# Flamingo layer, attention stage: masked maximum in one VectorE operation, scores in three passes over high and low halves, four probability buffers, new engine orders

## The reference

```python
xn = _ln(x, g_x, b_x)                        # also ln, from the latents (here x)
q = ln @ w_q
kv_in = jnp.concatenate([xn, ln], axis=1)    # 120 + 256 = 376 rows
k, v = jnp.split(kv_in @ w_kv, 2, axis=-1)
q, k, v = (split(q) * scale, split(k), split(v))
sim = jnp.einsum('bhid,bhjd->bhij', q, k)
sim = jnp.where(m, sim, -jnp.finfo(sim.dtype).max)   # m: the mask over the 120 context rows, True after them
attn = jax.nn.softmax(sim, axis=-1)
out = jnp.einsum('bhij,bhjd->bhid', attn, v)
return _ln(out @ w_out, g_o, b_o)
```

## Time and profile before

| | us |
|---|---|
| median of 3 runs | 2430.0 (2428.2 to 2432.1) |
| profiled execution, its own time | 2407.8 |
| span of the profiled execution | 2405.8 |
| PE, DVE, ACT, POOL busy | 2280, 1685, 1278, 1002 |

### The profile page before, as it was taken

One profiled execution on the slowest core, in us unless ns is written; L12 is line 12 of the kernel. 1 busy time (PEld: TensorE's weight loads), 2 busy tenths in 40 slices (PEclk: granted clock), 3 DMA queues, 4 the chain that ended last, 5 costly groups with the idle time before them and its releaser, 6 DMA issues. The chain is left out here.

```text
span 2405.8 us, 53171 instructions
## 1 busy us (share of the span) xinstructions
PE 2280.3 (95%) x15744; PEld 1885.0 (78%) x15744; DVE 1685.0 (70%) x5052; ACT 1278.3 (53%) x3249; POOL 1001.6 (42%) x1418
## 2 busy tenths in 40 slices
PE   4999999999999999999949999999789999999998
PEld 3777777777777777777649999999768888888887
DVE  2577676776767776777645555555378989898997
ACT  3666666666666666676523333333244445454554
POOL 1455555556556555555530000000155555555552
PEclk9999999999999999999979999999999999999999
DMA  7001001011010010010033222221122211111110
GB/s 279 19 28 36 26 29 37 18 35 33 22 36 27 27 36 26 29 37 13 22 118 105 80 80 80 80 80 45 57 67 59 60 58 59 58 58 58 58 48 19
DMA packets 111772, 128.97 MB, mean 54 GB/s; under 512 B 15058, under 2 KB 98505, under 8 KB 111424
## 3 DMA queue, kind: packets, MB, share of 16 engines
q1 hardware_dynamic: 99264, 105.42, 13.8%
q0 software_dynamic: 12288, 21.21, 3.1%
HBM read 84.42 MB, written 54.53 MB: 58 GB/s over the span
## 5 line engine op out<-in xcount | busy, mean ns | idle before, releaser
L367 POOL TENSOR_TENSOR a_prob<-a_prob,a_rden 128x752 f32<-128x752 f32 x256 | 369.0, 1442 | 321.1 <-DVE a_rden L647 300.1
L641 DVE TENSOR_REDUCE a_nmax<-a_score 128x1 f32<-128x376 f32 x512 | 270.7, 542 | 187.1 <-PE a_score L964 176.7
L496 ACT ACTIVATE a_prob<-a_score,a_nmax 128x376 f32<-128x376 f32 x512 | 292.6, 574 | 94.2 <-DVE a_nmax L641 94.2
L1292 ACT ACTIVATE e_hidden<-e_first,e_b 128x256 f32<-128x256 f32 x320 | 133.9, 471 | 287.2 <-PE e_first L80 283.9
L972 PE MATMUL a_turned<-a_ident,a_prob 128*128 128x128 f32 (+1 forms) x1536 | 238.0, 281 | 32.2 <-DVE a_probT L653 20.7
L972 PEld LDWEIGHTS a_turned<-a_ident,a_prob 128*128 128x128 f32 (+1 forms) x1536 | 170.9, 142 | 99.2 <-issue 57.3
L80 PE MATMUL e_first<-e_rowsT,e_w 128*128 128x256 f32 x1920 | 238.7, 285 | 1.6 <-issue 1.6
L80 PE MATMUL e_second<-e_w,e_hidden 128*128 128x256 f32 x1920 | 239.7, 285 | 0.0
L80 PEld LDWEIGHTS e_first<-e_rowsT,e_w 128*128 128x128 f32 x1920 | 235.0, 194 | 1.8 <-issue 1.8
L960 PE MATMUL a_score<-a_kT,a_qT 64*128 64x376 f32 x1024 | 231.9, 530 | 2.4 <-ACT a_prob L496 2.3
L80 PEld LDWEIGHTS e_second<-e_w,e_hidden 128*128 128x128 f32 x1920 | 232.7, 192 | 0.0
(11 more groups left out here) (203 smaller groups left out, 4859.5 us busy)
## 6 DMA issues: line engine op xcount, KB each, us to landing
slots<-a_y SPq DMA_DIRECT2D x8, 1280.0 KB, 14.3
e_rows<-slots SPq DMA_DIRECT2D x40, 256.0 KB, 4.0
answers<-e_y SPq DMA_DIRECT2D x40, 256.0 KB, 2.3
a_xn<-x SPq DMA_DIRECT2D x32, 256.0 KB
w_in<-W SPq DMA_DIRECT2D x16, 512.0 KB, 3.9
a_xr<-x SPq DMA_DIRECT2D x32, 256.0 KB, 2.9
x<-a_x SPq DMA_DIRECT2D x32, 256.0 KB, 3.1
e_w_in<-W SPq DMA_DIRECT2D x16, 512.0 KB, 4.1
```

Source lines behind the costliest of these rows:

```text
L367: nc.gpsimd.tensor_tensor(prob[:, u % 4], prob[:, u % 4], rden[:, u % 4].unsqueeze(2).to_broadcast([P, 2, NKV]), ALU.mult) \
L496: nc.scalar.activation(prob[:, u % 4, a], score[SCORE_AT[u][a]][:, 0:NKV], ACT.Exp, bias=nmax[:, u % 4, a:a + 1], accum_out=den[:, u % 4, ...
L641: nc.vector.tensor_reduce(nmax[:, u % 4, a:a + 1], score[SCORE_AT[u][a]][:, 0:NKV], AX.X, ALU.max, negate=True).then_inc(nmax_ok[a], 1)
L1292: nc.scalar.activation(hidden[:, 2 * j + i], first[:, j, i * CH:(i + 1) * CH], ACT.Relu, bias=b1[:, 2 * j + i, bass.ds(e, 1)]).then_inc(re ...
```

## The change

- Keys and queries get two planes, high and low, in fp32r. ACT writes the high one as before, DVE the low one with two new functions, `k_low` (four per batch, 128x376) and `q_low` (two per batch, 128x512). What waited for `k_hi` and `q_hi` on PE now waits for `k_lo` and `q_lo`.
- `scores` makes three fp32r passes per head in place of one f32 matmul, the heads in turn; the bf16 matmul for the mask and `firstrow` go.
- The mask row is f32, 376 wide, zero beyond the context. `row_max` becomes one `tensor_tensor_reduce`: it adds the mask to the scores, negates, writes the result to `prob` in SBUF and its minimum to `nmax`. `exps` then reads `prob` (scale -1) and not PSUM. So the score bank is free after `row_max`, and `scores` waits for `nmax_ok` and not for `exp_ok`; `row_max`, which now writes the buffer, waits for the transposes of the unit four earlier, as `exps` did.
- The orders in `step` are new on PE, DVE, ACT and POOL. Among it: `turn_x` is done for batch s at the end of step s, not for s - 1 near the start; `times_v` of pair 2 moves from the end of a step to behind the scores of unit 2 in the next; on DVE `stat` moves forward, `logits_shift` into the next step, `place` forward, and `over_sum(s - 1, 0)` from the end of a step into the next, which makes `logits_in` the last operation of a step; on ACT `standardise` moves forward; on POOL `norm0` moves forward and `dispatch` ahead of the eighth `normalise`.

```diff
@@ -146,8 +145,8 @@
         xh = sb("a_xh", [P, 3, D])
         kvin = sb("a_kvin", [P, KD, NKV])
         kvin2 = sb("a_kvin2", [P, 2, 2, KD, NKV], F32R)
-        qT = sb("a_qT", [P, 2, KI, S])
-        kT = sb("a_kT", [P, 2, KI, NKV])
+        qT = sb("a_qT", [P, 2, 2, KI, S], F32R)
+        kT = sb("a_kT", [P, 2, 2, KI, NKV], F32R)
         vo = sb("a_vo", [P, 2, 3, KI, 2, DH])
...
                 eng.wait_ge(nmax_ok[a], NG * b + u + 1)
-                at_least(eng, turned_ok[a], NG * b + u - 3)
-                nc.scalar.activation(prob[:, u % 4, a], score[SCORE_AT[u][a]][:, 0:NKV], ACT.Exp,
-                                     bias=nmax[:, u % 4, a:a + 1],
+                nc.scalar.activation(prob[:, u % 4, a], prob[:, u % 4, a], ACT.Exp,
+                                     bias=nmax[:, u % 4, a:a + 1], scale=-1.0,
                                      accum_out=den[:, u % 4, a:a + 1]).then_inc(exp_ok[a], 1)
 
...
+            def k_low(b, p, m):
+                eng.wait_ge(k_hi, KI * b + m + 1)
+                nc.vector.tensor_tensor(kT[:, p, 1, m], work[0][:, 0:NKV], kT[:, p, 0, m].bitcast(F32),
+                                        ALU.subtract).then_inc(k_lo, 1)
+
+            def q_low(b, p, i):
+                eng.wait_ge(q_hi, 2 * b + 2 - i)
+                pair = slice(2 * i, 2 * i + 2)
+                nc.vector.scalar_tensor_tensor(qT[:, p, 1, pair], work[1][:].rearrange("p (m s) -> p m s", m=2),
+                                               DH ** -0.5, qT[:, p, 0, pair].bitcast(F32),
+                                               ALU.mult, ALU.subtract).then_inc(q_lo, 1)
+
             def mask_line(b, p):
+                if isinstance(b, int) and b == 0:
+                    eng.wait_ge(small_in, 16 * N_SMALL)
                 for a in range(2):
-                    at_least(eng, score_ok[a], NG * (b - 1))
-                nc.vector.tensor_scalar(mask_row[:, p], mask_u8[:, bass.ds(b, 1)].rearrange("p o c -> p (o c)"),
+                    at_least(eng, nmax_ok[a], NG * (b - 1))
+                nc.vector.tensor_scalar(mask_row[:, p, 0:C], mask_u8[:, bass.ds(b, 1)].rearrange("p o c -> p (o c)"),
                                         -1.0, MASKED, ALU.add, ALU.mult).then_inc(mrow_ok, 1)
 
-            def row_max(b, u, a):
-
+            def row_max(b, p, u, a):
+
+
+                at_least(eng, turned_ok[a], NG * b + u - 3)
+                if u == 0:
+                    eng.wait_ge(mrow_ok, b + 1)
                 eng.wait_ge(score_ok[a], NG * b + u + 1)
-                nc.vector.tensor_reduce(nmax[:, u % 4, a:a + 1], score[SCORE_AT[u][a]][:, 0:NKV], AX.X,
-                                        ALU.max, negate=True).then_inc(nmax_ok[a], 1)
+                by_itself(eng, waited)
+                nc.vector.tensor_tensor_reduce(prob[:, u % 4, a], score[SCORE_AT[u][a]][:, 0:NKV], mask_row[:, p],
+                                               -1.0, 3.0e38, ALU.add, ALU.min,
+                                               nmax[:, u % 4, a:a + 1]).then_inc(nmax_ok[a], 1)
...
             def step(s, p):
...
+                if live(s - 2):
+                    row_max(s - 2, p, 1, 1)
                 if live(s - 3):
                     turned_out(s - 3, 6, 1)
                 if live(s - 2):
-                    row_max(s - 2, 1, 1)
-                    row_max(s - 2, 2, 0)
+                    row_max(s - 2, p, 2, 0)
+                    over_sum(s - 2, 0)
+                    row_max(s - 2, p, 2, 1)
                 if live(s - 3):
                     att_low(s - 3, 2)
                     turned_out(s - 3, 7, 1)
-                if live(s - 1):
-                    mask_line(s - 1, q)
-                if live(s - 2):
+                if live(s - 2):
+                    row_max(s - 2, p, 3, 1)
+                    row_max(s - 2, p, 3, 0)
                     over_sum(s - 2, 1)
...
                 if live(s - 4):
                     place(s - 4, p)
-                if live(s - 1):
-                    row_max(s - 1, 1, 0)
+                if live(s - 2):
+                    att_low(s - 2, 1)
+                    turned_out(s - 2, 4, 1)
+                if live(s - 1):
+                    row_max(s - 1, q, 0, 0)
+                    k_low(s - 1, q, 2)
+                if live(s):
+                    mask_line(s, p)
+                if live(s - 1):
+                    row_max(s - 1, q, 0, 1)
+                if live(s - 2):
+                    turned_out(s - 2, 5, 1)
+                    over_sum(s - 2, 7)
+                if live(s - 1):
+                    row_max(s - 1, q, 1, 0)
                 if live(s - 3):
                     logits_in(s - 3)
-                    logits_shift(s - 3)
-                if live(s - 1):
-                    over_sum(s - 1, 0)
...
 
                 m, i = u // 2, u % 2
-                if u == 0:
-                    eng.wait_ge(mrow_ok, b + 1)
                 if i == 0:
-                    eng.wait_ge(k_hi, KI * b + m + 1)
-                    eng.wait_ge(q_hi, 2 * (b + 1))
-                at_least(eng, exp_ok[0], NG * b + u)
-                at_least(eng, exp_ok[1], NG * b + u - 1)
-                for a in range(2):
-                    rows = slice(64 * a, 64 * a + 64)
-                    nc.tensor.matmul(score[SCORE_AT[u][a]][:, 0:NKV], qT[rows, p, m, i * P:(i + 1) * P],
-                                     kT[rows, p, m], start=True, stop=False)
-                for a in range(2):
-                    rows = slice(64 * a, 64 * a + 64)
-                    nc.tensor.matmul(score[SCORE_AT[u][a]][:, 0:C], firstrow[rows], mask_row[rows, p],
-                                     start=False, stop=True).then_inc(score_ok[a], 1)
+                    eng.wait_ge(k_lo, KI * b + m + 1)
+                    eng.wait_ge(q_lo, 2 * (b + 1))
+                at_least(eng, nmax_ok[0], NG * b + u)
+                at_least(eng, nmax_ok[1], NG * b + u - 1)
+                for w, (plane_q, plane_k) in enumerate(PASSES):
+                    for a in range(2):
+                        rows = slice(64 * a, 64 * a + 64)
+                        made = nc.tensor.matmul(score[SCORE_AT[u][a]][:, 0:NKV],
+                                                qT[rows, p, plane_q, m, i * P:(i + 1) * P], kT[rows, p, plane_k, m],
+                                                start=w == 0, stop=w == len(PASSES) - 1)
+                        if w == len(PASSES) - 1:
+                            made.then_inc(score_ok[a], 1)
...
                 if live(s - 2):
                     scores(s - 2, p, 2)
                 if live(s - 3):
+                    times_v(s - 3, q, 2)
+                    turn_prob(s - 3, 7, 0)
+                if live(s - 2):
+                    scores(s - 2, p, 3)
+                if live(s - 3):
                     turn_prob(s - 3, 7, 1)
-                    turn_prob(s - 3, 7, 0)
-                if live(s - 2):
+                if live(s - 2):
+                    project_k(s - 2, p, 3)
+                if live(s - 1):
+                    turn_c(s - 1)
+                if live(s - 2):
+                    turn_prob(s - 2, 0, 0)
+                    turn_prob(s - 2, 0, 1)
                     project_v(s - 2, p, 1)
-                if live(s - 1):
-                    turn_c(s - 1)
-                    turn_x(s - 1)
-                if live(s - 2):
-                    turn_prob(s - 2, 0, 1)
-                    scores(s - 2, p, 3)
-                    turn_prob(s - 2, 0, 0)
+                    scores(s - 2, p, 4)
                 if live(s - 3):
                     times_v(s - 3, q, 3)
...
+                    turn_prob(s - 2, 4, 0)
+                if live(s - 1):
+                    project_k(s - 1, q, 2)
                     scores(s - 1, q, 0)
-                if live(s - 2):
-                    turn_prob(s - 2, 4, 0)
+                    project_v(s - 1, q, 2)
+                if live(s - 3):
+                    router_turn(s - 3, q)
+                if live(s - 2):
                     turn_prob(s - 2, 5, 1)
-                if live(s - 3):
-                    router_turn(s - 3, q)
-                if live(s - 1):
-                    project_v(s - 1, q, 2)
-                if live(s - 2):
                     turn_prob(s - 2, 5, 0)
+                if live(s - 1):
+                    scores(s - 1, q, 1)
+                if live(s):
+                    turn_x(s)
+                if live(s - 3):
+                    router_logits(s - 3)
+                if live(s - 2):
+                    turn_prob(s - 2, 6, 0)
                     turn_prob(s - 2, 6, 1)
-                if live(s - 1):
-                    scores(s - 1, q, 1)
-                if live(s - 3):
-                    router_logits(s - 3)
-                if live(s - 2):
-                    turn_prob(s - 2, 6, 0)
-                if live(s - 1):
-                    project_k(s - 1, q, 2)
-                if live(s - 2):
```

(1 more changed line is left out.)

197 lines of the change are left out of this document (103 added, 94 removed).

## The result

| | before | changed | ratio (95%) |
|---|---|---|---|
| first comparison | 2431.1 us | 2460.8 us (2454.9 to 2464.2) | 1.0118 (1.0105 to 1.0131) |
| the same two kernels on another chip | 2407.2 us | 2402.4 us (2397.1 to 2404.1) | 0.9978 (0.9966 to 0.9991) |

The account below looks back on a forecast made before the run. Stage one was taken to run at PE's pace. Twelve loop rounds gave -47 us, eleven jumps +33, eight other batches -14: -28 from 2430.0, so 2402 us; range 2366 to 2450, the forecast's own 2382 to 2425.

Parts of the forecast that it names:

- PE, the scores: Score matmuls on PE: three fp32r passes per unit at 0.62 us, saving 0.265 per unit, 2.1 per batch, 68 over 256 units.
- rival D: Score matmuls on PE: fp32r halves of the array don't pair, +2.7 us per batch, 2550 us in all; chance 0.04.
- at most 0.64: Score unit on PE: highest time in us if two heads run side by side and the first pass's extra 0.1 isn't halved.
- Small waits: PE waits because DVE is level with it: +0.3 us per loop round, +0.4 per batch outside the loop.
- DVE, the work: DVE per round of the loop: k_low and q_low add 6.4 us, the new row maximum 1, giving 59.7 from 52.3.
- Rival B: DVE's new row-maximum operation runs at half rate, +0.4 us each, 6.4 per batch: 2520 to 2550 us; chance 0.07.
- The rule which I weighed: DVE's new row maximum: by its letter the half-throughput rule doesn't apply, having only one SBUF source, so the sum stays.
- DVE at the jump: Where the rolled loop jumps back: PE idles 3.7 us for DVE instead of 1.7, +2.0 per jump, 11 jumps.
- The clock: PE's clock halves after long waits at the loop's jumps: 1.0 us lost per jump on average, between 0 and 1.7.
- POOL: Dispatch ahead of the eighth normalise, four DMAs of 1.0 us each: covered mostly, and the jump hides it.
- The base: Differences worked out on the profiled execution, 2407.8 us, but subtracted from the runs' median, 2430.0 us.
- C: DVE level with PE, each handing over late, 0.4 us of PE waiting per unit: 2435 to 2480 us; chance 0.13.

## Why the prediction was wrong

The pace of a step, from the lines above, taken apart:

| us per step | late: before, changed | prompt: before, changed |
|---|---|---|
| written out, no scatter | 35.80, 35.01 | 35.80, 35.00 |
| scatter | 0.02 to 0.15, 1.25 | not run, 0.10 |
| the rest in the loop: jump, half of it per step, and what else differs from written out | 1.4, 2.1 | about 0.7, 1.2 |
| in the loop | 37.3, 38.4 | 36.5, 36.3 |

- **PE, the scores: right in kind, sized too high.** The halves pair also in fp32r, so rival D is out: the six passes start within 0.5 us.

```profile
L999 PE MATMUL a_score<-a_kT,a_qT x6: 329/332/434, 707.9 to 708.3; 64*128 64x376 f32 x6
```

```profile
707.87 0.78 PE L999 MATMUL a_score<-a_kT,a_qT 64*128 64x376 f32 x6
708.58 1.52 PE L1036 MATMUL a_values<-a_probT,a_vo 128*64 128x256 f32 x12
```

A unit takes 0.71 us from its start to the next work's, against 0.88: 0.17 saved, not 0.265; 1.4 per batch and 45 in all, not 68. The step that failed halved the whole 1.22 us of six full-height matmuls (its "at most 0.64" should read 0.66 by its own terms). Inside such a group a pass follows the one before by 0.17 us, and a pair of half-height passes does so too. But the second comes 0.27 or 0.28 us behind the first, and the next work of other height 0.26 behind the last, in both kinds of group: 0.28 + 0.17 + 0.26 is the 0.71. These 0.2 us at the two ends aren't halved. The Trainium skill, TensorEngine Tiling (Array Packing), Key Properties, says that changing the tiling mode drains the engine; this agrees in kind.

- **Small waits: too low.** I charged 0.15 to 0.4 us per batch. Written out, with or without the scatter, PE waits 0.77 in every step for one row maximum ahead of scores(6); in the rolled loop 0.58, once or twice per round. So written out 0.8 us per step are gained, not 2.1 less 0.4.

- **DVE, the work: the sum was right by luck, its parts weren't.** 60.4 us of 73 on the prompt chip against 59.7. By line and form, 400 to 1200 us, late chip, against the earlier trace rows:

```profile
L664 DVE CUSTOM_DVE_ANT_0 a_prob<-a_score,a_mask_row 128x376 f32<-128x376 f32 x336 | 178.9, 542 | 48.8 <-issue 30.1 <-PE a_score L999 17.7
...
L638 DVE TENSOR_TENSOR a_kT<-a_work,a_kT 128x376 fp32r<-128x376 f32 x84 | 45.4, 540 | 3.4 <-ACT a_kT L476 2.9
...
L644 DVE SCALAR_TENSOR_TENSOR a_qT<-a_work,a_qT 128x512 fp32r<-128x512 f32 x42 | 28.9, 687 | 16.2 <-ACT a_qT L483 16.2
L664 DVE DVE_READ_ACCUMULATOR2_ANT a_nmax<- 128x1 f32 x336 | 27.9, 83 | 5.8 <-issue 5.8
```

The new operation takes the 542 ns of the reduction it replaces, the read of its accumulator (83 ns) lies in what overlapped before, k_low was 540 for 544, q_low 687 for 759. Rival B is out. What I missed is that operations of the router that no diff line touches grew, and the row I used as B's upper bound was misread. Single lines, durations as least/median/most ns, L683 and L715 before, L707 and L739 (the same two operations) after:

```profile
L683 DVE SCALAR_TENSOR_TENSOR a_x<-a_y,a_rs,a_xb x64: 471/483/1672, 100.6 to 1220.1; 128x256 f32<-128x256 f32 x64
```

```profile
L715 DVE TENSOR_TENSOR a_lg<-a_lg,a_lmax x32: 174/175/176, 116.3 to 1228.7; 128x16 f32<-128x16 f32 x32
```

```profile
L707 DVE SCALAR_TENSOR_TENSOR a_x<-a_y,a_rs,a_xb x64: 472/482/961, 103.8 to 1263.7; 128x256 f32<-128x256 f32 x64
L739 DVE TENSOR_TENSOR a_lg<-a_lg,a_lmax x32: 176/1451/1455, 124.5 to 1272.3; 128x16 f32<-128x16 f32 x32
```

The 986 ns of L683 in the earlier trace rows are a mean over two kinds, 483 in the middle and up to 1672: no rate of two SBUF inputs, but waiting for POOL. L739 shows whom for:

```profile
692.74 1.45 DVE L739 TENSOR_TENSOR a_lg<-a_lg,a_lmax 128x16 f32<-128x16 f32 x1
```

```profile
692.72 1.44 POOL L366 TENSOR_TENSOR a_prob<-a_prob,a_rden 128x752 f32<-128x752 f32 x1 [0.57 <-DVE a_rden L671]
```

An operation of 16 columns with both inputs in SBUF starts 0.02 us behind POOL's normalise and ends when that has ended. The Trainium skill, SBUF — State Buffer, section Who interferes with whom, has an exclusive lock on the port pair that DVE and GpSimd share, and says that a DVE instruction with two SBUF inputs contends with a GpSimd instruction that reads SBUF; the trace agrees, 175 ns become 1451. The rule which I weighed, from the Trainium skill, Vector Engine (DVE) Microarchitecture Reference, section Points that are easy to get wrong, half throughput for an instruction like scalar_tensor_tensor with two non-bf16 SBUF sources, the trace doesn't bear out here: 483 ns, against 477 with one in PSUM. In `logits_shift` (L739) and `choose` (L757) the waiting is worth 1.2 + 0.5 us per batch more than before, ahead of the row maximum that PE waits 0.77 for, while L707 gives 0.6 back elsewhere in the step. That the wait comes from it is likely and was not tried.

- **DVE at the jump: right in mechanism, wrong in place and size.** I named times_v as the waiting work, for the copy turned_out(6, 1). But pair 2 is units 4 and 5, and times_v ran, with turn_prob(7, 0) behind it: 3.4 us of cover behind router_logits, not 1.35. What waits is scores(3), for the maximum of unit 2, third on DVE behind the jump. The two errors nearly cancel in the idle time on late chips (3.2 to 3.7 against 3.7 forecast), since the late completion comes on top; that hit is luck. On prompt chips it is 2.1 to 2.5, against 1.3 to 2.3 before. By the table a round grows by 2 x 0.7 = 1.4 and about 1.0 us, where I had 3.0 for a jump; part of the jump's growth comes back as shorter waits ahead of scores(6) than written out.

- **The clock: sized right on prompt chips** (0.9 us per jump against 1.0), and above my upper bound of 1.7 on late ones (2.6), since a stretch at 1.2 GHz can be 6.8 us long and the earlier trace rows showed one of 3.4.

- **POOL: the step that turned the sign.** I put dispatch at nothing: "covered mostly, and the jump hides it". I looked at POOL's own queue and not at who completes work while POOL issues DMAs. In the trace of before on which I worked completions weren't late at all. Written out it costs 1.25 us per step on late chips, some 40 over 32 batches, against 5 at most before; in the rolled loop PE waits 20.3 us for logits_in (250 to 1100 us), against 10.2 in the kernel before for the late row maximum, and the idle time at each jump is 1.2 us longer than on a prompt chip, with 1.7 us more lost to the clock behind it.

- **The base.** I took a difference off 2430, while the trace's own execution had 2408. On a prompt chip 28 us less would be 2379; measured was 2402.4. So the forecast also fails there, by 23 us. That the time there equals the forecast is chance. Added up again from the traces, as an estimate in us over stage one: on a prompt chip the scores give -45, the waits ahead of scores(6) +15 (7 forecast), the 11 jumps +19 (0.8 idle and 0.9 clock each; 33 forecast) and the scatter +3, together -8; measured was -5. On a late chip -45, +12, +45 (1.8 and 2.3 each) and +17 for late completions in the steps (27 less the old order's 10), together +29; measured was +30.

Of the rivals C came nearest: slower by order, with PE waiting for DVE once or twice per step. But it isn't DVE handing over each unit late. Without late completions the same order is 0.2% faster than the kernel before.

## What to carry to other kernels

When a step is moved, look for what is completed and waited for while another engine issues indirect DMAs, not only at the queue it moves in; and profile on more than one chip when the profiled time and the median differ by 1%. A mean duration of an operation with both inputs in SBUF is no rate until its least, median and longest agree (471, 483 and 1672 ns for L683, mean 986): where they don't, look at what GpSimd does then. In a rolled loop, work that is put last on the engine that stands longest at the jump moves that jump behind it; here writing the loop out was worth 1.2 to 1.3% (before), and 1.1% on a prompt chip (changed), more than the change itself. Of the two written-out kernels the one before is better on late chips (0.987 against 0.993). On prompt ones only the changed one was run with its scatter (0.987), so which is better there is not shown.
